# Routed results gathered plain and added on VectorE for six token tiles, in place for the other six, and the next group's row turns put behind a chunk's scores

## The reference, cut to what matters

```python
h = _L0_tok_ref(x, ...)                                        # (64, 23, 512)
h = h + _L0_attn_ref(_layernorm(h, axis=-1), ...)
h = h + _L0_ffn_ref(_layernorm(h, axis=-1), ...)               # 16 experts, top 4 of them per token, and one shared expert
h = h + _L1_attn_ref(_layernorm(h, axis=-1), Wq, Wk, Wv, Wo)   # 16 heads of 32, 4 kv heads, rope, causal softmax
h = h + _L1_ffn_ref(_layernorm(h, axis=-1), ...)               # ternary weights
```

## Time and profile before

| | us |
|---|---|
| median of three runs | 1510.72 (1509.34 to 1511.55) |
| the profiled execution | 1511.43 |
| its span in the profile | 1509.5 |
| PE / DVE / ACT / POOL busy | 1294.1 / 896.4 / 629.5 / 308.6 |

### The profile page before, as it was taken

One profiled execution on the slowest core, in us unless ns is written; L12 is line 12 of the kernel. 1 busy time (PEld: TensorE's weight loads), 2 busy tenths in 40 slices (PEclk: granted clock), 3 DMA queues, 4 the chain that ended last, 5 costly groups with the idle time before them and its releaser, 6 DMA issues.

```text
span 1509.5 us, 30358 instructions
## 1 busy us (share of the span) xinstructions
PE 1294.1 (86%) x10660; PEld 829.6 (55%) x10674; DVE 896.4 (59%) x1865; ACT 629.5 (42%) x1066; POOL 308.6 (20%) x336
## 2 busy tenths in 40 slices
PE   6878899999999999986759999999972868768997
PEld 3446677777777877764424444444531656424443
DVE  5776455555565555668653555544332665578886
ACT  3445344444444444442314444444431333236664
POOL 2443000000000000000012233333267853010000
PEclk9997999999999999996779999999995869789999
DMA  5111343524435352422315767865268520000000
GB/s 181 68 66 43 100 178 138 200 105 174 142 127 204 135 185 109 156 85 89 124 70 178 257 227 257 303 242 170 98 125 133 85 43 3 2 1 8 21 21 32
DMA packets 44238, 184.26 MB, mean 122 GB/s; under 512 B 8688, under 2 KB 9200, under 8 KB 36368
## 3 DMA queue, kind: packets, MB, share of 16 engines
q0 software_dynamic: 21280, 95.41, 20.3%
q1 hardware_dynamic: 19440, 75.41, 14.3%
q10 hardware_dynamic: 3456, 12.58, 2.3%
HBM read 135.65 MB, written 47.73 MB: 121 GB/s over the span
## 4 chain that ended last, share of the span: by engine, by line
PE 55%; DVE 18%; issue 13%; POOL 7%; ACT 4%; DMA 2%; DVEq 1%; ACTq 0%; POOLq 0%; SPq 0%
PE ps L929 14%; PE ps L931 13%; PE ps L930 13%; POOL h L506 3%; PE ps L1036 3%; PE ps L1019 3%; PE ps L1255 2%; DVE ff L1976 2%; DVE amf L1983 1%; PE ps L1120 1%; PE ps L1052 1%; POOL rt_out L466 1%; PE ps L1348 1%; PE ps L1366 1%; POOL qraw L539 1%
## 5 line engine op out<-in xcount | busy, mean ns | idle before, releaser
L929 PE MATMUL ps<-nT_hi,wa_hi 128*128 128x368 f16 x448 | 147.9, 330 | 11.8 <-DVE wa_lo L1395 8.1
L930 PE MATMUL ps<-nT_lo,wa_hi 128*128 128x368 f16 x448 | 147.3, 329 | 0.0
L931 PE MATMUL ps<-nT_hi,wa_lo 128*128 128x368 f16 x448 | 147.0, 328 | 0.1
L496 POOL DMA_INDIRECT xg<-xrow,idx x61 | 61.4, 1007 | 276.7 <-PE ps L1120 121.5
L1559 DVE TENSOR_TENSOR a<-sq,E 92x368 f32<-92x368 f32 x64 | 31.7, 534 | 136.3 <-ACT sq L694 136.3
L1731 DVE SCALAR_TENSOR_TENSOR nrm<-ps,xg,nrm 128x256 f32<-128x256 f32 x61 | 29.5, 484 | 133.3 <-ACT nrm L737 112.1
L930 PE MATMUL ps<-wa_lo,nT_hi 128*92 128x128 f16 (+1 forms) x560 | 107.1, 235 | 0.0
L929 PE MATMUL ps<-wa_hi,nT_hi 128*92 128x128 f16 (+1 forms) x560 | 107.1, 235 | 0.0
L931 PE MATMUL ps<-wa_hi,nT_lo 128*92 128x128 f16 (+1 forms) x560 | 107.1, 235 | 0.0
L929 PE MATMUL ps<-wide,xT 128*128 x244 | 93.6, 383 | 12.9 <-issue 8.2
L491 POOL DMA_DIRECT2D wsp<-we_sp x16 | 8.6, 539 | 446.6 <-DVE we_sp L1395 446.6
(11 more groups left out here) (302 smaller groups left out, 3326.1 us busy)
## 6 DMA issues: line engine op xcount, KB each, us to landing
we_st<-in_we POOLq DMA_DIRECT2D x16, 1536.0 KB, 6.8
wsp<-we_sp POOLq DMA_DIRECT2D x16, 1536.0 KB, 5.4
wide<-wsp SPq DMA_DIRECT2D x16, 1536.0 KB
yslot<-yt POOLq DMA_DIRECT2D x61, 256.0 KB
wq_st<-in_ffq SPq DMA_DIRECT2D x24, 512.0 KB, 6.0
wq_st<-in_ffq ACTq DMA_DIRECT2D x24, 512.0 KB
wide<-in_wa SPq DMA_DIRECT2D x10, 1024.0 KB, 4.8
xt<-in_x SPq DMA_DIRECT2D x12, 512.0 KB, 3.5
```

The lines of the kernel that those rows point to most:

```text
L496: pool.indirect_dma_start(Q["xg"][:, g % 4, :].bitcast(U32), None, xrow, bass.IndirectOffsetOnAxis(ap=idx[:, g:g + 1], axis=0)).then_inc(x ...
L929: nc.tensor.matmul(dst, lhs[0], rhs[0], start=start, stop=False)
L930: nc.tensor.matmul(dst, lhs[0], rhs[1], start=False, stop=False)
L931: return nc.tensor.matmul(dst, lhs[1], rhs[0], start=False, stop=stop)
```

## The change

POOL gets `collect(k)`: four plain gathers of tile k into a landing buffer of four rows per partition. DVE gets `returned(k)`: four additions of 128 x 512 floats which bring the four landed rows into `h`. Tiles 0 to 5 go this way. There are four landing buffers (three in the memory of the expert weights, one in that of the ternary weights); tiles 4 and 5 use the first two again, and so wait until `returned(0)` and `returned(1)` are done. Tiles 6 to 11 keep the gathers that add in place, in another order among POOL's other work. The row turns of all groups but the first are now behind the scores: for group 1 just ahead of the scores of chunk 0, for groups 2 and 3 behind the scores and the weighted sum of chunks 1 and 2. One more of the products with the sine goes from POOL to DVE (piece 3, in chunks 1 to 3).

```diff
@@ buffers
+        landing = [flat[:, 2048 * x:2048 * x + 2048].rearrange("p (j d) -> p j d", d=D) for x in range(3)]
+        landing += [wq_st[:].rearrange("p a b -> p (a b)")[:, 0:2048].rearrange("p (j d) -> p j d", d=D), landing[0], landing[1]]
@@ gpsimd
+            def collect(k):
+                if k > 3:
+                    pool.wait_ge(c_h, ready(NT + k - 4))
+                for j in range(TOPK):
+                    pool.indirect_dma_start(landing[k][:, j, :], None, yslot,
+                                            bass.IndirectOffsetOnAxis(ap=slot[:, k, j:j + 1], axis=0)).then_inc(sh_in[k], 16)
@@ gpsimd, cosine
-                if c and j < 4:
+                if c and j < 3:
@@ gpsimd, order
-            for j in range(TOPK):
-                shares(0, j)
-                shares(1, j)
+            for k in range(5):
+                collect(k)
+            turned_root(0)
+            collect(5)
             pool.wait_ge(m_y, VT)
             shares(2, 0)
-            turned_root(0)
+            cosine(0, 0)
+            cosine(0, 1)
             nc.gpsimd.memset(Fm["qp"][:, :, :, SL:], 0.0).then_inc(f_pad, 1)
-            shares(3, 0)
             turned_root(1)
-            cosine(0, 0)
-            shares(2, 1)
-            cosine(0, 1)
             cosine(0, 2)
-            shares(2, 2)
             cosine(0, 3)
             cosine(0, 4)
-            shares(2, 3)
+            shares(2, 1)
             pool.wait_ge(wa_lo, UNITS + 1)
             nc.gpsimd.memset(st_a[:], 0.0).then_inc(f_pad, 1)
+            shares(2, 2)
+            cosine(1, 0)
+            cosine(1, 1)
+            shares(2, 3)
+            for j in range(2, 5):
+                cosine(1, j)
+            turned_root(2)
+            shares(3, 0)
             shares(3, 1)
+            cosine(2, 0)
+            cosine(2, 1)
+            shares(3, 2)
+            cosine(2, 2)
+            shares(3, 3)
+            cosine(2, 3)
+            cosine(2, 4)
+            turned_root(3)
             for j in range(5):
-                cosine(1, j)
-            shares(3, 2)
-            turned_root(2)
-            shares(3, 3)
-            turned_root(3)
-            for c in range(2, CH):
-                for j in range(5):
-                    cosine(c, j)
+                cosine(3, j)
@@ scalar, after moved(0, 0), moved(0, 1); the new order whole
+            act.wait_ge(wa_in, 16 * (UNITS + 1))
+            nc.scalar.activation(wo[0][:]..., st_a[:], ACT.Copy, scale=WS).then_inc(wa_hi, 1)
             for c in range(CH):
                 k = GT * (c + 1)
+                for j in range(2, 6):
+                    moved(c, j)
+                if c:
+                    weights_turned(c - 1)
+                if c + 1 < CH:
                     normed(k)
                     normed(k + 1)
+                if c:
                     exponential(c)
                     y_high(c - 1)
+                if c + 1 < CH:
                     high(k)
                     normed(k + 2)
                     high(k + 1)
                     high(k + 2)
                     moved(c + 1, 0)
+                if c == 0:
+                    exponential(c)
+                if c + 1 < CH:
                     moved(c + 1, 1)
@@ tensor, the new order whole
                 for j in range(2, 6):
                     project(c, j)
                 if c:
                     turn(c - 1)
+                    scores(c)
+                    weighted(c - 1)
+                if c + 1 < CH:
+                    for j in range(GT):
+                        row_turn_l1(k + j)
                 if c == 0:
+                    scores(c)
+                if c + 1 < CH:
                     project(c + 1, 0)
                     project(c + 1, 1)
@@ vector
+            def returned(k):
+                y = landing[k]
+                dve.wait_ge(sh_in[k], SHARES[k] + 64)
+                dve.sem_inc(passed, 1)
+                V.tensor_tensor(y[:, 0, :], y[:, 0, :], y[:, 1, :], ALU.add)
+                order(V.tensor_tensor(y[:, 2, :], y[:, 2, :], y[:, 3, :], ALU.add))
+                order(V.tensor_tensor(row(k), row(k), y[:, 0, :], ALU.add))
+                V.tensor_tensor(row(k), row(k), y[:, 2, :], ALU.add).then_inc(c_h, 1)
             def total_stats(k):
-                dve.wait_ge(sh_in[k % 6], SHARES[k % 6] + 64 * (k // 6 + 1))
+                if k < 6:
+                    dve.wait_ge(c_h, ready(NT + k))
+                else:
+                    dve.wait_ge(sh_in[k % 6], SHARES[k % 6] + 128)
                 ...
             def group_stats(g):
                 for k in range(GT * g, GT * g + GT):
+                    if k < 6:
+                        returned(k)
                     total_stats(k)
                 ...
@@ vector, order: group_stats(0), group_shift(0), low(0..2), then
+            rotate(0, 0)
+            rotate(0, 1)
+            group_stats(1)
+            dve.wait_ge(wa_hi, UNITS + 1)
+            split_lo(wo[1][:]..., st_a[:], wo[0][:]..., wa_lo)
             for c in range(CH):
                 k = GT * (c + 1)
                 if c:
+                    rotate(c, 0)
+                    rotate(c, 1)
                     weights(c - 1)
                 for j in range(2, 5):
                     rotate(c, j)
+                if c == 0:
+                    group_shift(1)
                 rotated(c)
+                if 0 < c < CH - 1:
+                    group_stats(c + 1)
+                    group_shift(c + 1)
                 if c:
+                    centred(c)
                     y_low(c - 1)
+                if c + 1 < CH:
                     for j in range(GT):
                         low(k + j)
+                if c == 0:
+                    centred(c)
```

More of the change, by code:

```diff
@@ L820, in _ @@
             moved(0, 1)
+            act.wait_ge(wa_in, 16 * (UNITS + 1))
+            nc.scalar.activation(wo[0][:].rearrange("p a b -> p (a b)"), st_a[:], ACT.Copy, scale=WS).then_inc(wa_hi, 1)
             for c in range(CH):
                 k = GT * (c + 1)
-                if c % 2 == 0:
+                for j in range(2, 6):
[3 more added lines that the diff above has]
+                if c + 1 < CH:
                     normed(k)
                     normed(k + 1)
[L826 to L839, removed]
-                else:
-                    weights_turned(c - 1)
-                if c == 1:
-                    normed(k)
-                    normed(k + 1)
+                if c:
                     exponential(c)
                     y_high(c - 1)
+                if c + 1 < CH:
                     high(k)
@@ L851, in _ @@
                     moved(c + 1, 0)
+                if c == 0:
+                    exponential(c)
+                if c + 1 < CH:
                     moved(c + 1, 1)
-                else:
-                    if c + 1 < CH:
-                        moved(c + 1, 0)
-                        moved(c + 1, 1)
-                    exponential(c)
-                    if c:
-                        y_high(c - 1)
             weights_turned(CH - 1)
@@ L1299, in _ @@
                     project(c, j)
-                    if c % 2 == 0 and j < 5:
-                        row_turn_l1(k + j - 2)
                 if c:
                     turn(c - 1)
+                    scores(c)
[3 more added lines that the diff above has]
+                        row_turn_l1(k + j)
                 if c == 0:
+                    scores(c)
+                if c + 1 < CH:
                     project(c + 1, 0)
                     project(c + 1, 1)
-                scores(c)
-                if c == 1:
-                    weighted(c - 1)
-                    for j in range(GT):
-                        row_turn_l1(k + j)
-                if 0 < c < CH - 1:
-                    project(c + 1, 0)
-                    project(c + 1, 1)
-                if c > 1:
-                    weighted(c - 1)
             turn(CH - 1)
@@ L1821, in _ @@
             group_shift(0)
-            group_stats(1)
             def rotate(c, j):
@@ L1883, in _ @@
                 low(k)
-            group_shift(1)
+            rotate(0, 0)
+            rotate(0, 1)
+            group_stats(1)
+            dve.wait_ge(wa_hi, UNITS + 1)
+            split_lo(wo[1][:].rearrange("p a b -> p (a b)"), st_a[:], wo[0][:].rearrange("p a b -> p (a b)"), wa_lo)
             for c in range(CH):
                 k = GT * (c + 1)
-                rotate(c, 0)
-                rotate(c, 1)
                 if c:
+                    rotate(c, 0)
+                    rotate(c, 1)
                     weights(c - 1)
                 for j in range(2, 5):
-                    if c % 2 == 0:
-                        low(k + j - 2)
                     rotate(c, j)
+                if c == 0:
+                    group_shift(1)
                 rotated(c)
-                if c == 0:
-                    dve.wait_ge(wa_hi, UNITS + 1)
```

(15 more changed lines are left out.)

7 lines of the change are left out of this document (3 added, 4 removed).

## The result

The changed kernel took **1531.84 us** (median of four runs, 1530.56 to 1532.80), the kernel before 1511.13 beside it: ratio 1.0138, 95% interval 1.0120 to 1.0155. The sign was forecast, the size was not: +20.7 us where the sum said +10.4, and above the range (1512 to 1528). The profiled execution spans 1529.6 us, 20.1 more than before.

The account below looks back on a forecast made before the run. No engine is full: a chain of POOL's gathers, then the attention's chunk chain, bounds the kernel. Step changes -7.9 + 2.4 + 6.4 + 10.1 - 0.6 = +10.4 on the median 1510.72 give 1521.1 us, range 1512 to 1528.

Parts of the forecast that it names:

- the sum: Step changes up to the output projection: -7.9, +2.4, +6.4, +10.1 and -0.6, together +10.4 us.
- The first row: Group 0's first normalized row, ahead of the attention chunks: at 1141.3, 16.2 us earlier than before.
- DVE is not free before 1128.29: In the first rows: shared tiles and weight splits hold DVE until then; 11.8 us of its work follow to group 0's request.
- S0: Start of chunk 0's scores: forecast at 1178.9, 7.9 us earlier, with half of the 16.2 us given back.
- The chunk steps: From each chunk's scores to the next, last to the output projection: 29.1, 45.8, 38.0 and 23.4 us.
- S2: Start of chunk 2's scores: 1253.8, 0.9 us later, with POOL's gathers ahead of the pieces that `rotated` needs.
- S1: Start of chunk 1's scores: 1208.0, 5.5 us earlier, with three POOL gathers ahead of pieces 2 to 4.
- t + 11.2: Chunk 1's scores would start 11.2 us after t, its shuffle of piece 1, without three POOL gathers between the cosines.
- (1): Rival: DVE's additions lock POOL out, tile 4's gathers take 3.53 + 0.30 us each; 1528 us, 7 in 100.
- the page's rule weighed in the forecast: GpSimd contends with DVE instructions having two SBUF inputs, so every gather beside `returned` stalls.
- (2): Rival: POOL's gathers of groups 2 and 3 do not bind in the chunk steps, 12.6 us less; 1508.5 us, 5 in 100.
- (3): Rival: faster, as S1 to S2 was long for two groups' rows; turns behind scores under about 33 us; 1503, 8 in 100.
- the step S2 to S3: From chunk 2's scores to chunk 3's: 38.0 us where before 27.91; the moved turns alone cost 10 us.

Follow-up runs that it names:

- e2: Changed kernel with a 0.55 us memset behind each of the first 16 plain gathers, one every 1.68 us: 1521.59 us, ratio 1.0062 to the kernel before.
- e4: Changed order on all engines, but all 48 gathers add in place and DVE makes no additions: 1522.80 us, ratio 1.0076 to the kernel before.
- e5: Changed kernel with POOL's gathers for groups 2 and 3 moved ahead of the cosines of chunks 1 and 2: 1525.54 us, ratio 1.0079 to the kernel before.
- e14: Kernel before with plain gathers and additions for tiles 0 to 5, a 0.55 us memset behind each of the first 12 gathers: 1504.45 us, ratio 0.9955.
- e6: Changed kernel with group 3's turns back between chunk 2's projections, its gathers and root ahead of chunk 2's cosines: 1522.48 us, ratio 1.0066 to the kernel before.
- e8: Kernel before with group 0's in-place gathers first and its root among group 1's gathers: 1511.15 us, ratio 0.9989.
- e9: Kernel before with plain gathers and additions for tiles 0 to 5, the first 12 gathers paced by memsets, DVE's and POOL's orders rearranged: 1498.97 us, ratio 0.9917.
- e11: Changed kernel with a 0.55 us memset behind each of plain gathers 9 to 16 only: 1525.20 us, ratio 1.0092 to the kernel before.
- e15: Changed kernel with 96 waits on a long satisfied semaphore among PE's instructions ahead of the shared tiles: 1528.91 us (one run).
- e13: Changed kernel with the full-pace gather burst begun 5.6 us later, by a POOL wait until four shared additions are open: 1519.7 us (one run).
- e12: Changed kernel with a memset of 8 columns behind each of the first 16 plain gathers: 1532.65 us, ratio 1.0137 to the kernel before.
- e3: Kernel before, every order kept, with plain gathers and DVE additions for tiles 0 to 5: 1517.02 us, ratio 1.0036.
- e7: Changed kernel with each plain gather bringing half the bytes, 128 rows of 1 KB: 1531.32 us, ratio 1.0118 to the kernel before.
- e10: Changed kernel with each plain gather bringing half the rows, 64 of 2 KB: 1535.54 us, ratio 1.0158 to the kernel before.

## Why the prediction was right and wrong, step by step

**The first row: wrong, and this is the whole miss.** The step that failed is "DVE is not free before 1128.29 (shared tiles, weight splits), so from here DVE decides". I took that time over from the trace of before, where PE's last shared tiles ran beside adding gathers, and checked the plain ones against the DMA's bandwidth alone. Under the burst PE's signals came up to 11.2 us late, PE stood still for 8 us, and the last split ended at 1140.03, 11.7 late. The rest of the step holds: additions of 0.69 us as taken, a tile every 3.48 us (3.7 forecast), request 11.0 us behind the split (11.8 forecast), a gather every 1.26 us (1.27). Without the stall (e2) the first row stood at 1141.70 and the time at 1521.59, against 1141.3 and 1521.1 forecast. The term was not mis-sized, it was missing.

**S0: right from the first row on.** 37.6 us forecast from first row to S0, 37.1 measured; group 1's additions stand where the working put them, and half of what the first row wins is given back (e2: 15.8 us at the first row, 7.6 at S0).

**The chunk steps: right in sum, less so in their causes.** 29.1, 45.8, 38.0 and 23.4 forecast, 28.92, 45.22, 38.52 and 22.39 measured, and e4 has 28.95, 45.78 and 37.26 without a plain gather. At S2 the wait is the one named. At S1 it is not: `kr` starts at 1216.18 without a wait, and the time lies in a product of DVE that ran for 5.37 us beside POOL's products, so that 28.92 met 29.1 is in part luck. POOL and then DVE ahead of S2 in the changed kernel:

```profile
1256.07 1.55 POOL L515 DMA_INDIRECT h<-yslot,slot  x1 [0.31 <-issue]
1257.93 1.54 POOL L515 DMA_INDIRECT h<-yslot,slot  x1 [0.30 <-issue]
1258.92 2.45 POOL L548 TENSOR_TENSOR qraw<-qraw,cosT 128x368 f32<-128x368 f32 x2
```

```profile
1261.40 0.54 DVE L1852 TENSOR_TENSOR kr<-qraw,qs 128x368 f32<-128x368 f32 x1 [7.07 <-POOL qraw L548]
```

But taking those gathers out from between the cosines (e5) gave back 5.5 us and not 12.6, so "without the three gathers it would be t + 11.2" was too low: something else is late by then too.

**The rivals.** (1) did not come: tile 4's gathers beside the additions took 0.95 to 1.32 us, not 3.53. They are in the changed kernel's chain of waits:

```profile
1142.95 0.95 POOL wide L509
1144.20 1.32 POOL wide L509
1145.83 1.15 POOL wide L509
```

The contention shows on DVE's side instead: a product of 0.54 us took 5.37 beside POOL's products (1210.79 in the first fence). On the page's rule weighed in the forecast (the Trainium skill, GPSIMD Engine Reference, Key points): for such products the trace agrees; for additions beside gathers it shows at most 0.37 us more per gather, and the additions kept their 0.69. (2) was excluded by the trace and then halved by e5. (3) fell: the step S2 to S3, with one group's turns behind the scores, cost 38.52 us, above its 33.

**What was left out of the rivals** was one that the trace of before could not price but could have raised: the change packs 16 gathers into 19 us beside PE's last tiles, where before the same stretch held 11. A new rate on a shared resource is a term of its own, and it belongs into the range even where no row prices it. The runs did: 10.3 us in the changed order (e2), 12.6 in the order of before (e14).

## What to carry to other kernels

When a change speeds up a stream of DMA issues, price what the other engines do during it, and do not carry their times over from the slower stream: here 8 us of idle PE followed, and a gather every 1.67 us in place of 1.26 won 10 us. Move an order and the instructions that feed it one at a time, since a queue in program order hands a delay on to whatever then stands behind it (e5, e6, e8). A stage that comes earlier is worth only what the next queue lets through: 10.5 us of earlier first row were worth nothing in e8, and 16.7 were worth 12.5 in e9, where POOL's and DVE's queues were arranged for them.

## What the runs showed of the hardware

- **Where plain gathers were issued every 1.21 to 1.27 us beside PE's tiles, and a load of instructions passed behind six or seven of them, PE stood idle** for 8 to 12 us (seven kernels), whether a gather moved 256 KB or 128 KB and 128 rows or 64. With a gather every 1.67 or 1.68 us (five issued at the load) there was no gap; with seven issued and the slower pace after them (e11) it was 4.0 us. In e15 the burst lies against PE's work as in the changed kernel (its first gather 19.9 us ahead of the last shared addition, as in e2), only the load passes before it, and there is no gap. So the burst alone is not enough. That the load is the other half is not shown: e13 and e15 move the burst and PE's tiles as well, the records don't say that the load is PE's, and its packet itself is on time (0.9 us at 1113.68). Nor does the packet start it: in the changed kernel, e6, e11 and e12 PE's first late signal came 0.06 to 0.69 us before the packet began, and in e3 and e5 the matmuls behind that signal had ended 0.95 and 1.08 us before it. The Trainium skill, DMA: Bandwidth & Descriptors, Queues, rings and completion order, says that a DMA engine takes turns between its queues packet by packet; by that rule the load need not wait for the burst, and the trace agrees as far as the load's own packet goes. What then holds PE's signals back until the burst is almost over, and whether the gathers ahead of the load or the rate behind it matter, stays open.
- **What comes late is PE's signals** (8.3 and 11.2 us behind the recorded ends of the work, 0.01 in e2, e13 and e15). ACT waits for them 9.31 us, DVE behind ACT 11.69, and PE itself for ACT; POOL and the DMA go on; the wait appears as "issue" on PE and as "remote" on ACT, on a program that runs on one core.
- **The clock followed.** PE was idle from 1116.6; the clock stood at 1.00 to about 1122 (a mean of 0.87 over 1118 to 1123) and then at 0.50, TensorE's lower level of 1.2 GHz, at which the first matmuls behind the gap took 0.63 us in place of 0.38.
- **A plain gather costs 0.95 us and 0.30 of issue, and hardly less with half the bytes or half the rows** (e7, e10: 0.95 and 0.90), and a memset of 8 columns behind it costs nothing (1.27 us between gathers in place of 1.26).
